# Two loading queues deal out the four quarters of an adjacency granule in another order

## The reference

```
x = layernorm(x + L0(x, adj, a))
x = layernorm(x + L1(x, adj, w, a1, bias))
# L0:  e = leaky(src[:, None] + dst[None, :]);  e = where(adj > 0, e, -big)
#      softmax(e, axis=1) @ h
# L1:  the same with h = x @ w, and + bias behind it
```

## Time and profile before

| | us |
|---|---|
| median of 3 runs | 514.14 (512.53 to 514.8) |
| the profiled execution, its own time | 512.94 |
| its span, first to last instruction | 511.1 |
| PE busy / DVE busy / ACT busy in the span | 445.8 / 401.3 / 397.5 |
| POOL busy | 85.8 |
| adjacency loads, SP's queue | 64 DMAs of 512 KB, 9.4 us from issue to landing |
| adjacency loads, ACT's queue | 64 DMAs of 512 KB, 9.1 us from issue to landing |

### The profile page before, as it was taken

The page is one execution under the profiler, slowest core; times in us unless marked ns, Lnnn a source line. Parts: engine busy times, 40 slices in busy tenths (PEclk is TensorE's granted clock), DMA queues, the critical chain, the costliest instruction groups (busy, mean ns, idle before and its releaser), DMA issues.

```text
span 511.1 us, 11789 instructions
## 1 busy us (share of the span) xinstructions
PE 445.8 (87%) x4420; PEld 416.2 (81%) x4420; DVE 401.3 (78%) x712; ACT 397.5 (78%) x619; POOL 85.8 (17%) x68
## 2 busy tenths in 40 slices
PE   0799678979979798997969989999999999989891
PEld 0479668969978796997869869999999998989791
DVE  3679999889898998989887989775766657574854
ACT  2685279777998888789873749889898989898941
POOL 0002211415133051412403200000101010101010
PEclk9987978988999799898989859999999999999897
DMA  7999999999999999999953001102020111102000
GB/s 198 245 224 277 275 263 293 338 299 333 312 307 315 328 321 306 322 321 299 320 173 125 1 1 44 42 9 86 12 82 19 73 34 58 57 35 75 20 12 10
DMA packets 80294, 87.71 MB, mean 172 GB/s; under 512 B 7298, under 2 KB 76162, under 8 KB 80258
## 3 DMA queue, kind: packets, MB, share of 16 engines
q1 hardware_dynamic: 45602, 52.98, 36.3%
q10 hardware_dynamic: 34656, 34.21, 24.7%
HBM read 77.74 MB, written 9.44 MB: 171 GB/s over the span
## 4 chain that ended last, share of the span: by engine, by line
issue 50%; DVE 21%; DMA 21%; PE 3%; POOL 2%; SPq 1%; ACT 0%; POOLq 0%; ACTq 0%; DVEq 0%
DMA stage<-in_adj 19%; DVE narrow L791 5%; DVE turned L803 3%; PE acc L418 2%; DVE pos L817 2%; POOL small L968 2%; DMA xn<-in_x 2%; DVE num L861 1%; DVE num L854 1%; DVE red L847 1%; DVE kept L728 1%; DVE bn L866 1%; DVE kept L725 1%; DVE neg L820 1%; SPq L225 1%
## 5 line engine op out<-in xcount | busy, mean ns | idle before, releaser
L557 ACT ACTIVATE neg<-srow,dcol 128x512 int8 (+1 forms) x512 | 352.8, 878 | 11.7 <-issue 8.2
L418 PE MATMUL acc<-xy_old,pos 128*128 128x195 bf16 x1024 | 195.2, 260 | 26.3 <-POOL pos L979 22.1
L418 PE MATMUL acc<-xy_old,neg 128*128 128x195 bf16 x1024 | 195.0, 261 | 0.0
L418 PE MATMUL acc<-stage,pos 128*128 128x195 bf16 x1024 | 179.4, 249 | 4.8 <-DVE red L829 4.8
L418 PE MATMUL acc<-stage,neg 128*128 128x195 bf16 x1024 | 179.4, 249 | 0.0
L418 PEld LDWEIGHTS acc<-xy_old,pos 128*128 128x128 fp8e4 x1024 | 106.2, 104 | 34.8 <-issue 33.5
L418 PEld LDWEIGHTS acc<-stage,pos 128*128 128x128 fp8e4 x1024 | 101.2, 99 | 9.9 <-issue 9.7
L418 PEld LDWEIGHTS acc<-xy_old,neg 128*128 128x128 fp8e4 x1024 | 105.7, 103 | 1.4
L418 PEld LDWEIGHTS acc<-stage,neg 128*128 128x128 fp8e4 x1024 | 100.7, 98 | 0.2
L791 DVE TENSOR_SCALAR narrow<-stage 128x4096 uint8<-128x4096 int32 x32 | 74.0, 2314 | 17.7 <-DMA stage<-in_adj 16.9
L820 DVE TENSOR_TENSOR neg<-neg,kept 128x1024 uint32<-128x1024 uint32 x32 | 39.2, 1224 | 44.7 <-ACT neg L557 44.1
(11 more groups left out here) (117 smaller groups left out, 326.6 us busy)
## 6 DMA issues: line engine op xcount, KB each, us to landing
stage<-in_adj ACTq DMA_DIRECT2D x64, 512.0 KB, 9.1
stage<-in_adj SPq DMA_DIRECT2D x64, 512.0 KB, 9.4
spill<-turned SPq DMA_DIRECT2D x16, 512.0 KB, 8.1
turned<-spill SPq DMA_DIRECT2D x16, 512.0 KB, 3.9
out<-x1s SPq DMA_DIRECT2D x8, 128.0 KB, 1.9
xn<-in_x SPq DMA_DIRECT2D x1, 768.0 KB, 16.7
kept<-in_x SPq DMA_DIRECT2D x4, 128.0 KB, 3.8
kept<-in_x ACTq DMA_DIRECT2D x4, 128.0 KB, 4.6
```

The source lines that it names most:

```text
L418: last = nc.tensor.matmul(acc[:, r, c * XW:(c + 1) * XW], masks[c][:, t // BYTES, t % BYTES, r * P:(r + 1) * P], xy[layer][:, g * GT + t, ...
L557: last = nc.scalar.activation(o[:, t // BYTES, t % BYTES, :], srow[:, bass.ds((s % 2) * 512, 512)], ACT.Sign, bias=dcol[:, layer, col:col ...
```

## The change

The numbers of the quarters in two tuples change. Before, SP issues quarters 0 and 1 and ACT quarters 2 and 3. Now SP issues 0 and then 2, and ACT issues 3 and then 1.

```diff
-        LOWER, UPPER = (0, 1), (2, 3)
+        LOWER, UPPER = (0, 2), (3, 1)
 
         def load_tiles(queue, quarters):
             for a in quarters:
```

## The result

The changed kernel takes 528.92 us (median of 4 runs, 527.88 to 530.19) where the kernel before took 513.34 us beside it. The ratio is 1.030, 95% interval 1.026 to 1.034. The forecast was 529 us. The total was right; two of its terms were not, in opposite directions.

The account below looks back on a forecast made before the run. It took the continuous stream of adjacency loads as the bound, DVE close behind. The profiled 512.94 us plus 14.3 us of crossed time and 0.7 us at the start gave 528, with the median's 1.2 us 529; range 517 to 553 us.

Parts of the forecast that it names:

- The loads are a continuous stream that sets the period: From 61 to 257 us loads set the 29.9 us super-block, DVE close behind; a slower stream shows in full.
- the cost is absorbed: Rival: DVE's chain between its waits is the true bound, so only part of 15 us shows, 515 to 519 us; chance 0.05.
- The limit belongs to the half of the partitions, and not to the queue or to 32 partitions: Adjacency loads: 211 GB/s is what the partitions reached can take; both queues in one half share it.
- no cost in a crossed half: Rival: two transfers to different quarters of one half go at 336 GB/s, nothing changes, 514 us; chance 0.09.
- How long the queues are crossed: Both queues write one half for 19% of a quarter, 0.7 us at each border, 5.7 us in each super-block.
- the crossing locks in: Rival: the queues' gap grows to a whole quarter, 13 us more per super-block, 85 us, near 600 us; chance 0.11.
- What a crossed microsecond costs: Crossed time falls from 293 to 211 GB/s: 2.2 us more per super-block, 14.3 us over 6.5 super-blocks.
- faster: Rival: a queue running alone reaches both halves near a border and beats 211 GB/s, saving 4 us, 510 us; chance 0.05.
- The start: Before the long stretch, only ACT's first load for granule 1 was counted as slower: 0.7 us.
- the loads of x: At the start, 128 KB each; crossed, they may cost some tenths of a us, left out of the sum.
- ACT's first quarter of granule 1: Beside SP's second quarter from 22.9 to 26.7 us; in one half it takes 4.5 us for 3.8, 0.7 us more.
- DVE's work on the tables: From 31 to 61 us it is the chain, so it hides the crossed loads of granules 2 to 4.

Follow-up runs that it names:

- the experiment: Changed order in part of the kernel before: from the second super-block on 524.28 us; x loads and first super-block 517.79 us; x loads alone 515.00 us.
- the kernel with the partitions alone: Against the kernel before, partitions written in the changed order, pieces read from memory in the order of before: 527.82 us, ratio 1.029.

## Why the prediction was right, and where it was not

*The loads are a continuous stream that sets the period.* Right. 1 MB less in each super-block gave 8.1 us (513.35 to 505.23). From granule 4 to granule 31 DVE's waits for the loads grew from 14.5 to 24.3 us, by 9.8, which is all of the 9.9 us that this stretch grew. In the windows of the earlier trace rows they were predicted to reach 27 and reached 22.3. The rival "the cost is absorbed" falls with this: a slower load shows as a wait.

*The limit belongs to the half of the partitions, and not to the queue or to 32 partitions.* Right. It is shown three times: 209 GB/s for two even queues in the changed kernel, 212 in the kernel that keeps them in one half, and the cost follows the partitions alone. The rival "no cost in a crossed half" had the time of before, and falls. So does the rule of the Trainium skill beside it ("SBUF — State Buffer", "Can I just issue two DMAs to hit both halves?"), by which the pairing would not matter: two kernels that differ only in it took 514 and 582 us.

*How long the queues are crossed.* Predicted 19% from five borders. Counted over the whole stretch it is 23% before and 24% after. The five borders were a small sample and a little low. One of them was also misread: the 331 packets of SP in the earlier trace rows carry 0.48 MB, so some of them are the spill's, of 4 KB. Only 267 belong to the quarter, and the gap there is some 250 packets in place of 194, which makes the mean of the five 21%. But the changed order did not widen the gap: the mean is 159 packets before and 136 after. So the rival "the crossing locks in" did not come about.

*What a crossed microsecond costs.* This is the term that was mis-sized. 2.2 us for each super-block, 14.3 us in the stretch, were predicted; the traces have 9.9 us and the experiment 11.2 us, 1.5 to 1.7 us for each. The price came from a rate that falls to 211 GB/s for all of the crossed time. By the same count, of the loads' packets alone and without the spills, the crossed time with both queues active runs at 321 GB/s before and 248 after. The rate falls with the distance of both queues from a border. I took the crossed time in which both move evenly, now with all bytes: it runs at 287 GB/s where the nearer of the two is within 20 packets of a border, at 250 from 40 to 80 packets, at 226 from 80 to 120 and at 213 beyond. In the kernel before it is 316 to 333 at the same distances. So the price of 211 was right for time far from a border, and little of the crossed time is that: 5 of these 39 us lie beyond 80 packets. I think this is because 16 engines do not reach the border together, so that around it some write one half and some the other; no run isolates that.

The price was not the same in every super-block either. From granule 4 on, the first six took 29.3, 30.9, 29.5, 29.9, 30.3 and 29.8 us before, and 32.0, 32.9, 31.7, 30.7, 30.8 and 30.4 after. So the first three lost 2.0 to 2.7 us each, about the 2.2 predicted, and the other three 0.5 to 0.8. The crossed share fell too, from 34, 25 and 23% to 14, 19 and 20%.

There are two other effects. The time in which the two queues move evenly but are not counted as crossed also became slower, 312 to 283 GB/s. It is 116 us in the changed kernel, so by these rates it lost 116 x (1 - 283 / 312), some 11 us, beside the 39 x (1 - 248 / 321), some 9 us, of the crossed time (both are estimates). The prediction had this time at no cost. That a part of it is near a border for some engines would fit, and is not shown. Against this, the time in which one queue is nearly alone (under 35% of the packets for the other) fell from 82 to 59 us. This last is the place that the rival "faster" spoke of; the rate in it rose from 207 to 219 GB/s. It gives back less than the other two lose.

*The start.* This is the step that failed: 0.7 us predicted, 5.0 us in the trace, 4.0 us in the experiment. Four things are to be told apart.

First, the loads of x were set at some tenths and left out. DVE's first work on them starts 1.8 us later:

```profile
8.46 2.29 DVE L679 TENSOR_TENSOR kept<-kept 128x2048 f32<-128x2048 f32 x1 [6.51 <-DMA kept<-in_x]
```

```profile
10.30 2.29 DVE L679 TENSOR_TENSOR kept<-kept 128x2048 f32<-128x2048 f32 x1 [8.35 <-DMA kept<-in_x]
```

(the kernel before, then the changed one). Of this 1.2 us are left when granule 0 is narrowed, which waits for no load of its own in either kernel. The experiment has 1.5 us for the loads of x.

Second, ACT's first quarter of granule 1 is the term that was counted, and it was right. Nearly all of its packets run from 23.6 to 26.7 us before, and from 23.6 to 27.5 us after: 0.8 us more, where 0.7 was predicted.

Third, ACT's second quarter of granule 1, the last to land, was not counted, because the working ended at SP's second quarter. It takes 6.1 us in place of 3.4, so 2.7 us more, and this is the largest part. Towards its end it runs beside SP's first quarter of granule 2 in the same half: from 31 to 34 us both together move 218 GB/s, and only 110 of the 656 packets are ACT's. It is slow earlier too, 225 GB/s from 27.2 to 29 us, while the two are in opposite halves by the count; that is not explained. The second and the third together are 3.5 of the 3.6 us by which granule 1 is late.

Fourth, DVE's work on the tables was said to hide the rest up to 61 us. It hides the lateness of loads that have slack, but not that of granule 1, on which this work stands in line: those 3.6 us all reach granule 4, and 1.4 us come on top. Of these, 0.4 us are a wait for the load of granule 2, through which the chain now goes (16.18 us, up to 45.58). Another 0.9 us are its narrowing, which takes 3.2 us in place of 2.3, for a cause that was not looked into. In the trace of the kernel with the partitions alone this narrowing takes 2.3 us, and granule 4 comes at 64.63. So the 5.0 us of one trace is not firm to better than a microsecond or two, and the 4.0 us of the experiment are the better figure.

The two errors are 3.3 us too little at the start by the experiments and 3.1 us too much in the stretch. They cancel in the total, which was therefore better than its working: that it came within a microsecond is luck.

## What to carry to other kernels

Where two queues load at once and each transfer covers only some of the partitions, look at which partitions they write at the same time, and let each queue keep one half for itself: then no drift between them can bring them into the same one. An order that is right only while both are in step costs the more, the longer they are out of step: here 3.0%, with the queues crossed for some 24% of the stretch. A bound for such an effect is a window of the trace in which one queue is alone; count it in full only for stretches in which both queues stay in the one half, and less for short crossings.

## What the runs showed of the hardware

- Two queues writing different quarters of one half of the partitions share 209 to 212 GB/s in the windows shown; in opposite halves they reach 336 to 349 GB/s. Near a border between the halves the changed kernel runs in between, at 250 to 287 GB/s. One queue over all partitions reached 337.
- With the partitions held, the pieces of `adj` and of x that the two queues read at the same time could be paired otherwise without any difference (ratio 1.000, within 0.3%).
- The gap between the queues is not made by the spills: it is 150 and 154 packets with spills of 64 bytes a partition. It shrank from 136 to 84 packets when the DMAs were halved, and in the order of before from 159 to 90. Halving them in the order of before made the kernel 0.5% faster (interval 0.2 to 0.7%), where twice as many issues had been expected to cost something.
